# The state-space block's output projection merged with the norm, the turns and the routing logits that follow it

## The chip, the cores and the metric

The kernel runs on one core of one Trainium2 chip. The metric is the device time of one execution in microseconds (us). Five engines run their own instruction streams and meet at semaphores: PE (matmuls; PEld is its weight load, which overlaps it), DVE (vector), ACT (scalar), POOL (GpSimd) and SP (here it only issues DMAs).

## The reference, cut to what matters

Two layers act on x of 4 x 1024 tokens by 128 features. The second layer's first half is a state-space block, and its second half is a mixture of experts with 8 experts, of which each token takes 2. Around the change it computes:

```python
y = y * silu(z)                               # 256 inner features a token
out = y @ out_proj_w.T                        # 256 -> 128
out = out @ fc2_w.T + fc2_b                   # 128 -> 128
x = x + out
xn = layernorm(x)                             # over the 128 features, eps 1e-5
logits = xn @ gate_w.T + lb_bias              # 128 -> 8, then sigmoid, top 2
x = x + experts(xn, logits) + shared(xn)
```

## The kernel before, in words

All 4096 tokens stay in SBUF. `X` holds them with 128 tokens on the partitions, as 32 tiles of 128 features. `xnT` holds the normalized tokens turned, with the features on the partitions. The work goes by chunks of 512 tokens (4 tiles, one PSUM bank): `NCH` = 8 chunks, `CPB` = 2 chunks to a sequence of 1024 tokens, `TPC` = 4 tiles to a chunk, `TB` = 8 tiles to a sequence.

The program is a row of blocks. Each block gives every engine its list of instructions, and a block begins only when all engines have ended the one before. The last blocks are:

1. `mamba_scan` ends with two gates on DVE (L1907), which multiply the scan's sums by silu(z) into `m.u`.
2. `mamba_out`. PE multiplies the two output weights into one (L1960, `out_proj` by `fc2`), ACT copies the product to SBUF (L1974), and then PE makes each chunk's projection (L1967): 4 tiles x 2 halves of the inner features. In f32 each of these matmuls takes two passes, so a chunk has 16 of the trace's PE instructions. DVE adds a chunk to `X` (L1981) and takes its statistics, one `bn_stats` for each tile (L85). Two PSUM banks are used in turn. DVE runs in a loop over pairs of chunks.
3. `norm_transpose` of visit 2. SP issues the loads of the routing weights (L124, three tensors) and of the expert weights (three more). DVE turns the statistics of all 32 tiles into mean and variance + eps in seven small steps (L149 to L155). POOL raises the variance to the power -0.5 in eight pieces of 4 tiles (L134). DVE normalizes a chunk with four `tensor_scalar` (L164) into one of two halves of `xn`, PE turns it with four transposes (L177), and ACT copies the turned chunk to `xnT` (L209). One chunk behind, PE makes the routing logits of 8 columns (L183): 4 matmuls, 8 instructions in the trace.
4. `route_second` takes sigmoid and top 2 of the logits. Its first DVE instruction needs all of them, and stands in the next block.
5. `second_ffn` runs the experts, and ends the kernel.

In this part there is no planner: the order on each engine is the order in which the code above lists it. PE's and DVE's lists are worked in order, so that an instruction that waits holds up all that stand behind it.

In an earlier part of the kernel, between attention and the first layer's experts, the class `Front` already does a sum, statistics, moments, root and norm by sequence in straight code: L994 is its add, L85 its statistics, L1012 to L1022 its moments over 8 tiles, L984 the root of 8 tiles on POOL, L1030 the norm.

Of the kernel before, what the change touches and what calls it, by code (L numbers as in the profile page):

```python
# [11 lines left out]
ALU = mybir.AluOpType  # L12
# [76 lines left out]
LOGITS = 7  # L89


def norm_transpose(nc, g, visit, loads=(), load_x=False, route=None):

    with ExitStack() as ctx:
# [9 lines left out]
        steps_before = visit * STAT_STEPS  # L106
        if load_x:
            half_set, stats_ready = sem("half_set"), sem("stats_ready")
        if route is not None:
            logits_done = sem("logits_done")  # L110
        x_loaded = g.second_ring_in
        block = ctx.enter_context(nc.Block())

# [54 lines left out]
        @block.tensor  # L168
        def _(pe):
            pe.sem_inc(stored, TURNS)  # L170
            pe.wait_ge(g.consts_loaded, 32)

            def turn(c, k):
                pe.wait_ge(normed, chunks_before + c + 1)
                pe.wait_ge(stored, credits_before + c + 1)
                for j in range(TPC):
                    last = pe.transpose(PS[:, k, j * P:(j + 1) * P], xn[:, k, j, :], ident[:, :])  # L177
                last.then_inc(transposed, 1)

            def logits(c):  # L180
                pe.wait_ge(stored, credits_before + TURNS + c + 1)
                for n in range(c * TPC, (c + 1) * TPC):
                    last = pe.matmul(PS[:, LOGITS, n * n_experts:(n + 1) * n_experts], xnT[:, n * P:(n + 1) * P], route.gate_w[:, :],  # L183
                                     start=True, stop=True)
                last.then_inc(logits_done, 1)

            if route is None:
                with pe.Fori(0, NCH // TURNS) as i:
                    for k in range(TURNS):
                        turn(TURNS * i + k, k)  # L190
            else:

                n_experts = route.gate_w.shape[1]
                pe.wait_ge(route.loaded, route.all)
                for c in range(NCH):
                    turn(c, c % TURNS)
                    if c > 0:
                        logits(c - 1)
                logits(NCH - 1)
                pe.wait_ge(logits_done, NCH)  # L200

        @block.scalar
        def _(act):
# [701 lines left out]
class Front:  # L905
# [180 lines left out]
    def mix(self, pe, b, k):  # L1086
        c = CPB * b + k
        if c == 0:
            pe.wait_ge(self.wo_in, 16)
        if b == 2 and k == 0:  # L1090
            pe.wait_ge(self.route_steps, self.SCORES)
        if b >= 2 and k == 1:
            pe.wait_ge(self.added, c)
        if b == 3 and k == 0:
            pe.wait_ge(self.x_stored, c)
        pe.wait_ge(self.divided, c + 1)
        for j in range(TPC):
# [381 lines left out]
LOW_AT = (4 * NS, 6 * NS)  # L1479


def mamba_loads(nc, ctx, early, g):

    sb = lambda name, shape, dt=F32: ctx.enter_context(nc.sbuf_tensor(f"m_{name}", shape, dt))
    m = Loads(nc, ctx, "m_w")
    m.d = m.tensor("d", [P, DI], g.w["d"])
    m.last = Loads(nc, ctx, "mo_w")
    m.out_proj, m.fc2 = m.last.tensor("out_proj", [P, DI, P], g.w["out_proj"]), m.last.tensor("fc2", [P, E], g.w["fc2"])
    m.u, m.sz, m.dt = sb("u", [P, DI, N]), sb("sz", [P, DI, N]), sb("dt", [P, DI, N])
    m.dtu_turns = sb("dtu_turns", [P, NT, DI, P])  # L1490
# [12 lines left out]
    m.a_log = m.tensor("a_log", [P, DI, NS], g.w["a_log"])
    m.fc2_b = m.tensor("fc2_b", [P, E], g.w["fc2_b"].to_broadcast([P, E]))
    return m
# [435 lines left out]
                    pool.tensor_tensor(ch[:, half, :], decay_then_h(s, half), c_rows[:, s % C_RING, :], ALU.mult).then_inc(ch_ready, 1)  # L1941


def mamba_out(nc, g, m):

    with ExitStack() as ctx:
        sb = lambda name, shape, dt=F32: ctx.enter_context(nc.sbuf_tensor(f"mo_{name}", shape, dt))
        sem = lambda name: ctx.enter_context(nc.semaphore(f"mo_{name}"))
        X, PS = g.X, g.PS
        out_proj, fc2 = m.out_proj, m.fc2  # L1950
        w = sb("w", [P, DI, E])
        fused, w_ready, mixed, added, stats_ready = map(sem, ("fused", "w_ready", "mixed", "added", "stats_ready"))
        block = ctx.enter_context(nc.Block())

        @block.tensor
        def _(pe):
            pe.sem_inc(added, 2)
            pe.wait_ge(m.last.loaded, m.last.all)
            for half in range(DI):
                last = pe.matmul(PS[:, 2, half * E:(half + 1) * E], out_proj[:, half, :], fc2[:, :], start=True, stop=True)  # L1960
            last.then_inc(fused, 1)
            pe.wait_ge(w_ready, 1)
            for c in range(NCH):
                pe.wait_ge(added, c + 1)
                for j in range(TPC):
                    for half in range(DI):
                        last = pe.matmul(PS[:, c % 2, j * E:(j + 1) * E], m.u[:, half, c * CH + j * P:c * CH + (j + 1) * P], w[:, half, :],  # L1967
                                         start=half == 0, stop=half == DI - 1)
                last.then_inc(mixed, 1)

        @block.scalar
        def _(act):
            act.wait_ge(fused, 1)
            act.activation(w[:, :, :].rearrange("p a b -> p (a b)"), PS[:, 2, 0:DI * E], ACT.Copy).then_inc(w_ready, 1)  # L1974

        @block.vector
        def _(dve):
            def add(c, k):
                dve.wait_ge(mixed, c + 1)
                x = X[:, bass.ds(c * TPC, TPC), :]  # L1980
                dve.tensor_tensor(x, x, PS[:, k, :].rearrange("p (j e) -> p j e", e=E), ALU.add).then_inc(added, 1)  # L1981

            def stats(c):
                dve.wait_ge(added, 2 + c + 1)
                for j in range(TPC):
                    last = tile_stats(dve, g, c * TPC + j)
                last.then_inc(stats_ready, 1)

            with dve.Fori(0, NCH // 2) as i:
                for k in range(2):  # L1990
                    add(2 * i + k, k)
                    stats(2 * i + k)
            dve.wait_ge(stats_ready, NCH)

I2 = 64
PAIRS = NE // 2
# [267 lines left out]
def program(nc, w, out):  # L2264

    with ExitStack() as ctx:
        g = make_globals(nc, ctx, w, out)
        with ExitStack() as scope:
            first = first_loads(nc, scope, g)
            f = Front(nc, scope, g, first)  # L2270
            with ExitStack() as inner:
                weights = qkv_loads(nc, inner, g)
                norm_transpose(nc, g, 0, [weights], load_x=True)
                attention(nc, g, weights, f)
            first_ffn(nc, g, first, f)
        with ExitStack() as scope:
            with ExitStack() as early:
                m = mamba_loads(nc, scope, early, g)
                norm_transpose(nc, g, 1, [m, m.last])
                mamba_in(nc, g, m)  # L2280
            mamba_scan(nc, g, m)
            mamba_out(nc, g, m)
        with ExitStack() as scope:
            weights = second_loads(nc, scope, g)
            norm_transpose(nc, g, 2, [weights.route, weights], route=weights.route)
            route_second(nc, g, weights)
            second_ffn(nc, g, weights)

# [15 lines left out]
```

## Time and profile before

| | |
|---|---|
| median of 3 runs | 1384.82 us (1381.36 to 1385.63) |
| the profiled execution | 1387.3 us; span from first to last instruction 1385.5 us |
| mean granted TensorE clock | 0.933 |
| busy in the span | PE 1233.7, DVE 1089.5, ACT 851.2, POOL 575.9 us |
| last gate of the scan ends | 1215.02 us |
| last routing logits end | 1259.35 us |

Times are counted from the span's first instruction. "Idle before" in a timeline row, in square brackets, is how long the engine had stood idle before the row, and what ended that. "x16" is how many instructions the row merges. PEclk is the granted clock of TensorE: 1.00 is 2.4 GHz, 0.50 is 1.2 GHz. The first and third numbers of a windows row are the stretch and PE's busy time in it.

### The profile page before, as it was taken

The numbers are of one execution on the slowest core, as the hardware profiler recorded it, in microseconds if no ns is written. First come the engines' busy times: TensorE is split into PE (matmuls) and PEld (weight loads), VectorE is DVE, ScalarE is ACT, GpSimd is POOL, SyncE is SP. The second block draws the span as 40 slices with busy tenths as digits, with TensorE's granted clock in tenths as the row PEclk, the third lists the DMA queues.
The fourth block names the chain that finished last, engine by engine and source line by source line (L and its number), as shares of the span: only waits on it lengthen the run. The fifth ranks groups of instructions, "written<-read, shape, count | busy, mean of one in ns | idle before, by whom it ended". The sixth has DMA issues, their size and how long they took to land. (4 is left out here: it accounts for less than half of the span.)

```text
span 1385.5 us, 23363 instructions
## 1 busy us (share of the span) xinstructions
PE 1233.7 (89%) x8438; PEld 647.1 (47%) x8438; DVE 1089.5 (79%) x1318; ACT 851.2 (61%) x1506; POOL 575.9 (42%) x428
## 2 busy tenths in 40 slices
PE   4948999999899979899996966999999999976998
PEld 2412343333334435344443334655655556564665
DVE  4778999999799546856554867999999999864554
ACT  2524999999798633232222778989999899612221
POOL 2330000100111147666575024988888888820000
PEclk9966999999999889999996986999999999985999
DMA  4331112311211154332450001322222222110221
GB/s 112 103 126 43 55 51 66 104 57 52 79 43 43 42 125 139 97 103 94 117 103 22 0 6 48 106 92 92 100 99 92 92 99 100 61 29 22 63 62 38
DMA packets 70525, 103.16 MB, mean 74 GB/s; under 512 B 12598, under 2 KB 42246, under 8 KB 70422
## 3 DMA queue, kind: packets, MB, share of 16 engines
q1 hardware_dynamic: 69126, 100.47, 24.2%
q10 hardware_dynamic: 1296, 1.33, 0.3%
q8 instruction: 64, 1.05, 0.3%
q14 instruction: 39, 0.32, 0.1%
HBM read 88.00 MB, written 13.37 MB: 73 GB/s over the span
## 5 line engine op out<-in xcount | busy, mean ns | idle before, releaser
L646 DVE TENSOR_REDUCE att_found<-PS 128x2 f32<-128x1024 f32 (+2 forms) x288 | 333.0, 1219 | 15.1 <-PE PS L755 13.5
L722 ACT ACTIVATE att_prob<-PS 128x512 f32<-128x512 f32 x576 | 313.5, 596 | 44.5 <-PE PS L777 32.7
L1941 POOL TENSOR_TENSOR ms_ch<-xnT,ms_c_rows 128x1024 f32<-128x1024 f32 x103 | 243.9, 2369 | 45.1 <-PE PS L1851 33.1
L1851 PE MATMUL PS<-ms_ch,ident_sb 128*128 128x512 f32 x512 | 241.2, 593 | 0.9 <-POOL ms_ch L1941 0.9
L1902 DVE TENSOR_TENSOR_SCAN xnT<-xnT,PS 128x1024 f32<-128x1024 f32 x103 | 231.1, 2268 | 7.4 <-PE PS L1842 7.1
L1880 ACT ACTIVATE ms_scaled<-m_dtu_turns,m_bt 128x256 f32<-128x256 f32 x448 | 191.5, 495 | 29.3 <-PE PS L1842 29.3
L796 PE MATMUL PS<-att_prob,att_v 128*32 128x256 f32 (+1 forms) x2560 | 185.3, 376 | 2.8 <-ACT fr_out L711 2.6
L1842 PEld LDWEIGHTS PS<-ident_sb,ms_scaled 128*128 128x128 f32 x1024 | 120.5, 143 | 80.2 <-DVE xnT L1902 37.4
L1842 PE MATMUL PS<-ident_sb,ms_scaled 128*128 128x128 f32 x1024 | 136.8, 278 | 9.7 <-ACT ms_scaled L1880 4.6
L755 PE MATMUL PS<-kr,qr 55*128 55x128 bf16 (+4 forms) x1152 | 121.2, 291 | 25.2 <-DVE att_found L646 13.4
L1270 ACT ACTIVATE f_h<-PS,e_w_b 128x512 f32<-128x512 f32 x64 | 44.0, 687 | 140.7 <-PE PS L1421 137.4
L777 PE MATMUL PS<-qr,kr 55*128 55x128 bf16 (+4 forms) x1152 | 116.0, 279 | 10.3 <-ACT att_prob L722 7.4
L1851 PEld LDWEIGHTS PS<-ms_ch,ident_sb 128*128 128x128 f32 x512 | 87.3, 190 | 64.6 <-issue 61.2
L1887 ACT ACTIVATE xnT<-m_dt,m_a 128x1024 f32<-128x1024 f32 x103 | 116.8, 1135 | 0.0
L1251 POOL TENSOR_TENSOR f_yT<-f_yT,f_prod 128x512 f32<-128x512 f32 x56 | 71.1, 1269 | 75.2 <-DVE f_prod L1363 73.8
L755 PEld LDWEIGHTS PS<-kr,qr 48*128 48x128 bf16 (+1 forms) x1152 | 39.3, 96 | 133.6 <-issue 94.0
L1353 DVE SCALAR_TENSOR_TENSOR f_x3s<-PS,e_w_b,f_mask_row 128x512 f32<-128x512 f32 x64 | 48.0, 750 | 62.7 <-PE PS L1425 62.0
L1239 POOL TENSOR_TENSOR f_xm<-xnT,f_gate_row 128x512 f32<-128x512 f32 x64 | 81.2, 1271 | 11.4 <-DMA f_gate_row<-gate_rows_dram 7.5
L796 PEld LDWEIGHTS PS<-att_prob,att_v 128*32 128x32 f32 x2560 | 55.2, 109 | 64.1 <-issue 54.1
L1430 PE MATMUL PS<-f_h,e_w_w 128*128 128x512 f32 x128 | 66.3, 600 | 8.5 <-DVE f_prod L1363 8.4
L1421 PE MATMUL PS<-f_xm,e_w_w 128*128 128x512 f32 x128 | 67.6, 611 | 5.8 <-POOL f_xm L1239 5.8
L605 POOL TENSOR_TENSOR att_neg<-att_zero,att_row_max 128x32 f32<-128x32 f32 x16 | 4.1, 254 | 164.7 <-DVE att_row_max L659 164.7
(225 smaller groups left out, 1749.6 us busy)
## 6 DMA issues: line engine op xcount, KB each, us to landing
ms_c_rows<-bc_rows_dram SPq DMA_DIRECT2D x64, 512.0 KB, 3.6
f_gate_row<-gate_rows_dram SPq DMA_DIRECT2D x64, 256.0 KB, 3.4
f_mask_row<-mask_rows_dram SPq DMA_DIRECT2D x64, 128.0 KB, 3.1
qk_parts_dram<-parts SPq DMA_DIRECT2D x48, 128.0 KB, 1.9
heads_dram<-fr_out SPq DMA_DIRECT2D x16, 256.0 KB, 2.7
f_mask_row<-mask_rows_dram SPq DMA_DIRECT2D x64, 64.0 KB, 3.3
qr<-qk_parts_dram SPq DMA_DIRECT2D x32, 96.0 KB
qr<-qk_parts_dram SPq DMA_DIRECT2D x96, 32.0 KB
```

The costliest lines, as they stand in the source:

```text
L646: dve.tensor_reduce(found[:, :, pair, first:first + (n - 1) * step + 1:step], PS[:, bank:bank + 2, :].rearrange("p r (w n) -> p r w n", w= ...
L722: act.activation(prob[:, step % PROB_RING * GH + h, :], PS[:, SCORE_BANK + unit % SCORE_RING, :], ACT.Exp, scale=float(D) ** -0.5).then_in ...
L755: last = pe.matmul(PS[:, MAX_BANK + 2 * (m % 2) + r, at:at + n], rows(qr, count, i, pair, r, q_block * P, P), rows(kr, count, i, pair, r, ...
L777: last[r] = pe.matmul(PS[:, SCORE_BANK + (unit + r) % SCORE_RING, col:col + w], rows(kr, count, i, pair, r, j * P, P), rows(qr, count, i, ...
L796: last = pe.matmul(PS[VW * h:VW * (h + 1), VALUE_BANK, q - half * CH:q - half * CH + w], v1[:, i % 2, half, h, j, :], prob[:, step % PROB_ ...
L1239: pool.tensor_tensor(xm[:, e % XM_RING, :], xnT[:, c * CH:(c + 1) * CH], gate_row[:, e % ROW_RING, :], ALU.mult).then_inc(xm_ready, 1)
L1842: last = pe.transpose(PS[:, X_BANK + 2 * half + k // TPC, k % TPC * P:(k % TPC + 1) * P], scaled[:, s % 2, k, half, :], g.ident[:, :])
L1851: last = pe.matmul(PS[:, Y_BANK + 2 * half + q, :], g.ident[:, :], ch[:, half, q * CH:(q + 1) * CH], start=n == 0, stop=n == NS - 1)
L1880: last = act.activation(scaled[:, s % 2, i, :, :], m.dtu_turns[:, TB * b + i, :, :], ACT.Identity, scale=m.bt[:, at:at + 1])
L1887: act.activation(decay_then_h(s, half), m.dt[:, half, sequence(b)], ACT.Exp, scale=m.a[:, half, n:n + 1]).then_inc(decay_ready, 1)
L1902: dve.tensor_tensor_scan(decay_then_h(s, half), decay_then_h(s, half), inputs(half), 0.0, ALU.mult, ALU.add).then_inc(scanned, 1)
L1941: pool.tensor_tensor(ch[:, half, :], decay_then_h(s, half), c_rows[:, s % C_RING, :], ALU.mult).then_inc(ch_ready, 1)
```

## The change

`mamba_out` and `norm_transpose` of visit 2 become one block. The old visit-2 norm and its logits are no longer called, and `norm_transpose` loses its logits branch.

- **PE** runs, by steps 0 to 7, the projections of `BACK_MIXES` (chunks 0, 1, 2, 3 in step 0, then 4, 5, 6, 7 in steps 1 to 4), then the step's turn, then the logits of the chunk before. A projection of chunk c waits until chunk c-2 has been added to `X`.
- **DVE** runs in straight code: add and statistics of chunk c; after each second chunk the seven moment steps of that sequence (8 tiles, three of them without a wait behind them); then the norm of `BACK_NORMS`, which stands two chunks behind. After step 7 the norms of chunks 6 and 7 follow.
- **POOL** takes the root of one sequence's 8 tiles at a time: four instructions in place of eight.
- **ACT** copies each turned chunk to `xnT`, without the table load that the old norm began with.
- **SP** issues the six weight loads at the start of the merged block.
- The scan's tensors `sz`, `dt`, `dtu_turns`, `a` and `bt` are released before the merged block, so that the second layer's expert weights find room there.

```diff
+BACK_MIXES = [(0, 1, 2, 3), (4,), (5,), (6,), (7,), (), (), ()]
+BACK_NORMS = [(), (), (0,), (1,), (2,), (3,), (4,), (5,)]
...
+            def mix(c):
+                pe.wait_ge(w_ready, 1)
+                if c >= 2:
+                    pe.wait_ge(added, c - 1)
+                for j in range(TPC):
+                    for half in range(DI):
+                        last = pe.matmul(PS[:, c % 2, j * E:(j + 1) * E], m.u[:, half, c * CH + j * P:c * CH + (j + 1) * P], fused_w[:, half, :],
+                                         start=half == 0, stop=half == DI - 1)
+                last.then_inc(mixed, 1)
+
+            def turn(c):
+                pe.wait_ge(g.normed, norms_before + c + 1)
+                if c >= 2:
+                    pe.wait_ge(g.stored, turns_before + c - 1)
+                for j in range(TPC):
+                    last = pe.transpose(PS[:, TURN_BANK + c % 2, j * P:(j + 1) * P], xn[:, c % 2, j, :], g.ident[:, :])
+                last.then_inc(g.transposed, 1)
...
             for c in range(NCH):
-                pe.wait_ge(added, c + 1)
...
+                for ahead in BACK_MIXES[c]:
+                    mix(ahead)
+                if c == 1:
+                    pe.wait_ge(route.loaded, route.all)
+                turn(c)
+                if c >= 1:
+                    logits(c - 1)
+            logits(NCH - 1)
+            pe.wait_ge(logits_done, NCH)
...
+        @block.gpsimd
+        def _(pool):
+            for b in range(B):
+                pool.wait_ge(g.stat_steps, steps_before + STAT_STEPS * (b + 1))
+                pool.tensor_tensor(rstd[:, b % 2, :], tmp[:, 3, :], g.half[:, 0:TB], ALU.pow).then_inc(g.rstd_ready, 1)
...
+            for c in range(NCH):
+                add(c)
+                if c % CPB == CPB - 1:
+                    moments(c // CPB)
+                for ready in BACK_NORMS[c]:
+                    normalize(ready)
+            for c in (6, 7):
+                normalize(c)
...
-            mamba_scan(nc, g, m)
-            mamba_out(nc, g, m)
-        with ExitStack() as scope:
+                mamba_scan(nc, g, m)
             weights = second_loads(nc, scope, g)
-            norm_transpose(nc, g, 2, [weights.route, weights], route=weights.route)
+            mamba_out(nc, g, m, weights)
             route_second(nc, g, weights)
```

## Rows read from the trace of the kernel before

**Rows 1.** The page: its span, and the head of the chain that ended last.

```profile
span 1385.5 us, 23363 instructions
...
PE 8%; issue 0%; DVE 0%; PEldq 0%; DVEq 0%
```

**Rows 2.** Timeline of 1213 to 1260 us: start, length, engine, line, work, idle before.

```profile
1213.80 1.22 DVE L1907 TENSOR_TENSOR m_u<-PS,m_sz 128x1024 f32<-128x1024 f32 x1 [1.08 <-PE PS L1851]
...
1216.87 14.56 PE L1967 MATMUL PS<-mo_w,m_u 128*128 128x128 f32 x128 [0.47 <-ACT mo_w L1974]
1219.09 0.69 DVE L1981 TENSOR_TENSOR X<-X,PS 128x512 f32 x1 [4.07 <-PE PS L1967]
...
1234.61 0.33 SPq L124 DMA_DIRECT2D r_w_gate_w<-gate  x1
...
1234.76 0.21 DVE L149 TENSOR_TENSOR norm_tmp<-stats 128x32 f32<-128x32 f32 x1 [0.61 <-PEq L1946]
...
1236.43 8.09 POOL L134 TENSOR_TENSOR norm_rstd<-norm_tmp,half 128x4 f32<-128x4 f32 x8 [24.70 <-DVE norm_tmp L155]
...
1237.81 2.28 DVE L164 TENSOR_SCALAR norm_xn<-X,norm_mean,norm_rstd 128x128 f32 x8 [1.47 <-POOL norm_rstd L134]
...
1239.18 2.08 PE L177 MATMUL PS<-ident_sb,norm_xn 128*128 128x128 f32 x8 [7.76 <-DVE norm_xn L164]
...
1252.38 0.90 PEld L177 LDWEIGHTS PS<-ident_sb,norm_xn 128*128 128x128 f32 x4
...
1254.83 0.90 PEld L177 LDWEIGHTS PS<-ident_sb,norm_xn 128*128 128x128 f32 x4
...
1255.93 3.42 PE L183 MATMUL PS<-r_w_gate_w,xnT 128*128 128x8 f32 x16
```

**Rows 3.** Timeline of 447 to 457 us, DVE and then POOL: the like in the front.

```profile
447.77 0.69 DVE L994 TENSOR_TENSOR X<-X,PS 128x512 f32<-128x512 f32 x1 [1.81 <-PE PS L1098]
...
449.28 0.67 DVE L994 TENSOR_TENSOR X<-X,PS 128x512 f32<-128x512 f32 x1
...
450.89 0.17 DVE L1012 TENSOR_TENSOR fr_moments_tmp<-stats 128x8 f32<-128x8 f32 x1
...
454.19 2.14 DVE L1030 TENSOR_SCALAR fr_xn<-X,fr_mean,fr_rstd 128x128 f32<-128x128 f32 x8 [1.90 <-POOL fr_rstd L984]
...
452.43 1.65 POOL L984 TENSOR_TENSOR fr_rstd<-fr_moments_tmp,half 128x8 f32<-128x8 f32 x1 [5.69 <-DVE fr_moments_tmp L1022]
```

**Rows 4.** Windows: stretch, busy time of PE, PEld, DVE, ACT, POOL, PEclk, DMA, GB/s.

```profile
1216.00:1231.00 15.00, 14.53 (x130) 14.34 (x129) 10.32 (x31) 0.39 (x1) 0.00 (x0) 1.00 0.00 1
1236.00:1237.00 1.00, 0.00 (x0) 0.00 (x0) 0.31 (x2) 0.00 (x0) 0.57 (x1) 0.52 0.19 9
1240.00:1259.00 19.00, 19.00 (x94) 18.66 (x92) 6.78 (x25) 4.78 (x8) 4.52 (x5) 0.50 0.04 16
```

**Rows 5.** Timeline of PE at 585, 590, 788 and 861 us: bursts after a pause.

```profile
585.75 1.10 PE L1430 MATMUL PS<-f_h,e_w_w 128*128 128x512 f32 x2 [2.21 <-DVE f_prod L1363]
...
590.04 1.18 PE L1430 MATMUL PS<-f_h,e_w_w 128*128 128x512 f32 x2 [1.89 <-DVE f_prod L1363]
...
788.01 2.93 PE L1731 MATMUL PS<-xnT,mi_w_in_x 128*128 x4 [2.03 <-ACT mi_xc L1597]
...
861.48 2.87 PE L1842 MATMUL PS<-ident_sb,ms_scaled 128*128 128x128 f32 x12 [0.20 <-ACT ms_scaled L1880]
```

**Rows 6.** Windows beside rows 5: granted clock (PEclk) in the stretches there.

```profile
586.00:589.00 3.00, 2.15 (x8) 0.79 (x7) 3.00 (x4) 0.60 (x1) 2.24 (x2) 1.00 0.40 129
591.00:594.00 3.00, 3.00 (x5) 1.35 (x4) 1.44 (x2) 0.00 (x0) 3.00 (x4) 0.50 0.32 108
789.00:792.00 3.00, 3.00 (x5) 1.35 (x4) 3.00 (x7) 2.24 (x5) 0.00 (x0) 0.50 0.00 0
793.00:796.00 3.00, 3.00 (x8) 1.32 (x7) 3.00 (x7) 1.93 (x5) 0.00 (x0) 1.00 0.00 0
864.00:865.00 1.00, 1.00 (x5) 0.57 (x4) 1.00 (x2) 1.00 (x2) 1.00 (x1) 1.00 0.00 0
```

More of the change, by code:

```diff
@@ L89, with norm_transpose @@
 LOGITS = 7
-def norm_transpose(nc, g, visit, loads=(), load_x=False, route=None):
+def norm_transpose(nc, g, visit, loads=(), load_x=False):
     with ExitStack() as ctx:
@@ L108, in norm_transpose @@
             half_set, stats_ready = sem("half_set"), sem("stats_ready")
-        if route is not None:
-            logits_done = sem("logits_done")
         x_loaded = g.second_ring_in
@@ L178, in turn @@
                 last.then_inc(transposed, 1)
[L180 to L200, printed above, removed]
+            with pe.Fori(0, NCH // TURNS) as i:
+                for k in range(TURNS):
+                    turn(TURNS * i + k, k)
         @block.scalar
@@ L1479, with mamba_loads @@
 LOW_AT = (4 * NS, 6 * NS)
-def mamba_loads(nc, ctx, early, g):
+def mamba_loads(nc, ctx, scan, early, g):
     sb = lambda name, shape, dt=F32: ctx.enter_context(nc.sbuf_tensor(f"m_{name}", shape, dt))
@@ L1488, in mamba_loads @@
     m.out_proj, m.fc2 = m.last.tensor("out_proj", [P, DI, P], g.w["out_proj"]), m.last.tensor("fc2", [P, E], g.w["fc2"])
-    m.u, m.sz, m.dt = sb("u", [P, DI, N]), sb("sz", [P, DI, N]), sb("dt", [P, DI, N])
+    m.u = sb("u", [P, DI, N])
+    sb = lambda name, shape, dt=F32: scan.enter_context(nc.sbuf_tensor(f"m_{name}", shape, dt))
+    m.sz, m.dt = sb("sz", [P, DI, N]), sb("dt", [P, DI, N])
     m.dtu_turns = sb("dtu_turns", [P, NT, DI, P])
@@ L1941, in _, with mamba_out @@
                     pool.tensor_tensor(ch[:, half, :], decay_then_h(s, half), c_rows[:, s % C_RING, :], ALU.mult).then_inc(ch_ready, 1)
-def mamba_out(nc, g, m):
+BACK_MIXES = [(0, 1, 2, 3), (4,), (5,), (6,), (7,), (), (), ()]
+BACK_NORMS = [(), (), (0,), (1,), (2,), (3,), (4,), (5,)]
+def mamba_out(nc, g, m, w):
     with ExitStack() as ctx:
@@ L1948, in mamba_out @@
         sem = lambda name: ctx.enter_context(nc.semaphore(f"mo_{name}"))
-        X, PS = g.X, g.PS
+        X, PS, xnT, stats, route = g.X, g.PS, g.xnT, g.stats, w.route
         out_proj, fc2 = m.out_proj, m.fc2
-        w = sb("w", [P, DI, E])
-        fused, w_ready, mixed, added, stats_ready = map(sem, ("fused", "w_ready", "mixed", "added", "stats_ready"))
-        block = ctx.enter_context(nc.Block())
+        fused_w = sb("w", [P, DI, E])
+        tmp = sb("tmp", [P, 4, TB])
+        mean, rstd = sb("mean", [P, 2, TB]), sb("rstd", [P, 2, TB])
@@ new lines, in mamba_out, with _ @@
+        xn = sb("xn", [P, 2, TPC, E])
+        fused, w_ready, mixed, added, stats_ready, logits_done = map(sem, ("fused", "w_ready", "mixed", "added", "stats_ready", "logits_done"))
+        visit = 2
+        steps_before, roots_before, norms_before = visit * STAT_STEPS, visit * NCH, visit * NCH
+        turns_before = visit * (NCH + TURNS)
+        FUSED_BANK, TURN_BANK = 2, 3
+        block = ctx.enter_context(nc.Block())
+        @block.sync
+        def _(sp):
+            for group in (w.route, w):
+                for dst, src in group.pairs:
+                    sp.dma_start(dst, src).then_inc(group.loaded, 16)
@@ L1955, in _ @@
         @block.tensor
         def _(pe):
-            pe.sem_inc(added, 2)
+            def mix(c):
[7 more added lines that the diff above has]
+                last.then_inc(mixed, 1)
@@ new lines, in turn, with logits @@
+            def turn(c):
[5 more added lines that the diff above has]
+                last.then_inc(g.transposed, 1)
+            def logits(c):
+                pe.wait_ge(g.stored, turns_before + c + 1)
+                n_experts = route.gate_w.shape[1]
+                for n in range(c * TPC, (c + 1) * TPC):
+                    last = pe.matmul(PS[:, LOGITS, n * n_experts:(n + 1) * n_experts], xnT[:, n * P:(n + 1) * P], route.gate_w[:, :], start=True, stop=True)
+                last.then_inc(logits_done, 1)
@@ L1958, in _ @@
             pe.wait_ge(m.last.loaded, m.last.all)
             for half in range(DI):
-                last = pe.matmul(PS[:, 2, half * E:(half + 1) * E], out_proj[:, half, :], fc2[:, :], start=True, stop=True)
+                last = pe.matmul(PS[:, FUSED_BANK, half * E:(half + 1) * E], out_proj[:, half, :], fc2[:, :], start=True, stop=True)
             last.then_inc(fused, 1)
-            pe.wait_ge(w_ready, 1)
             for c in range(NCH):
-                pe.wait_ge(added, c + 1)
[L1965 to L1969, printed above, removed]
+                for ahead in BACK_MIXES[c]:
+                    mix(ahead)
@@ L1973, in _, with add @@
             act.wait_ge(fused, 1)
-            act.activation(w[:, :, :].rearrange("p a b -> p (a b)"), PS[:, 2, 0:DI * E], ACT.Copy).then_inc(w_ready, 1)
+            act.activation(fused_w[:, :, :].rearrange("p a b -> p (a b)"), PS[:, FUSED_BANK, 0:DI * E], ACT.Copy).then_inc(w_ready, 1)
+            for c in range(NCH):
+                act.wait_ge(g.transposed, turns_before + c + 1)
+                act.activation(xnT[:, c * CH:(c + 1) * CH], PS[:, TURN_BANK + c % 2, :], ACT.Copy).then_inc(g.stored, 1)
+            act.wait_ge(g.stored, turns_before + NCH)
+        @block.gpsimd
[3 more added lines that the diff above has]
+                pool.tensor_tensor(rstd[:, b % 2, :], tmp[:, 3, :], g.half[:, 0:TB], ALU.pow).then_inc(g.rstd_ready, 1)
         @block.vector
         def _(dve):
-            def add(c, k):
+            def add(c):
                 dve.wait_ge(mixed, c + 1)
[L1980 to L1984, printed above, removed]
+                x = X[:, c * TPC:(c + 1) * TPC, :]
+                dve.tensor_tensor(x, x, PS[:, c % 2, :].rearrange("p (j e) -> p j e", e=E), ALU.add).then_inc(added, 1)
+                dve.wait_ge(added, c + 1)
                 for j in range(TPC):
@@ L1987, in stats, with moments, normalize @@
                 last.then_inc(stats_ready, 1)
[L1989 to L1993, printed above, removed]
+            def moments(b):
+                steps = Steps(dve, g.stat_steps, steps_before + STAT_STEPS * b)
+                me, qe, mo, qo = (stats[:, TB * b:TB * (b + 1), k] for k in (1, 2, 4, 5))
+                dve.wait_ge(stats_ready, CPB * (b + 1))
+                if b > 0:
+                    dve.wait_ge(g.rstd_ready, roots_before + b)
+                steps.mark(dve.tensor_tensor(tmp[:, 0, :], me, mo, ALU.add))
+                steps.mark(dve.tensor_tensor(tmp[:, 1, :], me, mo, ALU.subtract))
+                steps.done(dve.tensor_tensor(tmp[:, 2, :], qe, qo, ALU.add))
+                steps.done(dve.scalar_tensor_tensor(tmp[:, 1, :], tmp[:, 1, :], 0.25, tmp[:, 1, :], ALU.mult, ALU.mult))
+                steps.mark(dve.scalar_tensor_tensor(tmp[:, 2, :], tmp[:, 2, :], 1.0 / E, tmp[:, 1, :], ALU.mult, ALU.add))
+                steps.done(dve.tensor_scalar(mean[:, b % 2, :], tmp[:, 0, :], 0.5, None, ALU.mult))
+                steps.done(dve.tensor_scalar(tmp[:, 3, :], tmp[:, 2, :], EPS, None, ALU.add))
+            def normalize(c):
+                b = c // CPB
+                dve.wait_ge(g.rstd_ready, roots_before + b + 1)
+                if c >= 2:
+                    dve.wait_ge(g.transposed, turns_before + c - 1)
+                for j in range(TPC):
+                    n = c % CPB * TPC + j
+                    last = dve.tensor_scalar(xn[:, c % 2, j, :], X[:, c * TPC + j, :], mean[:, b % 2, n:n + 1], rstd[:, b % 2, n:n + 1],
+                                             ALU.subtract, ALU.mult)
+                last.then_inc(g.normed, 1)
+            for c in range(NCH):
+                add(c)
[5 more added lines that the diff above has]
+                normalize(c)
+            dve.wait_ge(g.normed, norms_before + NCH)
 I2 = 64
@@ L2276, in program @@
         with ExitStack() as scope:
[L2277 to L2280, printed above, removed]
-            mamba_scan(nc, g, m)
-            mamba_out(nc, g, m)
-        with ExitStack() as scope:
+            with ExitStack() as scan:
+                with ExitStack() as early:
+                    m = mamba_loads(nc, scope, scan, early, g)
+                    norm_transpose(nc, g, 1, [m, m.last])
+                    mamba_in(nc, g, m)
+                mamba_scan(nc, g, m)
             weights = second_loads(nc, scope, g)
-            norm_transpose(nc, g, 2, [weights.route, weights], route=weights.route)
+            mamba_out(nc, g, m, weights)
             route_second(nc, g, weights)
```

## The prediction

> **What bounds the kernel now.** I read the page first. The span is 1385.5 us, and the chain that ended last lies wholly in the last block: its steps are PE's, 8% of the span [rows 1]. The blocks before it are joined by barriers, so the chain cannot be followed back through them. But for the same reason each block's length counts in full. So the second view is the timeline from the scan's last gate to the last routing logits, which are the two ends between which the change works. The gate ends at 1213.80 + 1.22 = 1215.02, the logits at 1255.93 + 3.42 = 1259.35 [rows 2]. The stage takes 44.3 us, 3.2% of the span, and nothing outside it is touched.
>
> The reader should see three parts in it. First the projections: PE's 128 passes in 14.56 us, 0.114 us each and 1.82 us a chunk, with DVE's add starting 2.22 us after its chunk [rows 2]. PE is through at 1231.4. Then a stretch in which PE has nothing: 7.76 us, in which the last statistics, the barrier, the moments, the first root and the first norm follow one another [rows 2]. Then turns and logits, PE busy for 19.00 of 19 us. The third view, windows, tells why this part is long: the granted clock was 1.00 during the projections, fell to 0.52 in the microsecond from 1236, in the pause, and stood at 0.50 from 1240 to 1259 [rows 4]. So 19 us of such work at 1.2 GHz did not bring 2.4 GHz back. A chunk of turn and logits takes 1254.83 - 1252.38 = 2.45 us [rows 2], where 12 passes at the full clock's 0.114 would take 1.37.
>
> **The change part by part.** I count from the gate's end, t = 0. What is removed: one barrier (0.61 us of idle before L149), the pause of PE, and seven moment steps on 32 columns. What is added: moments four times on 8 columns, and roots of 8 tiles. Their prices come from the front's rows, the same work in straight code [rows 3]. Add and statistics of a chunk: 449.28 - 447.77 = 1.51 us, 1.61 ahead of moments; I take 1.6. Moments: 1.54 from the first step to the root, of which 0.1 is the hand-over; three waits fewer leave 1.3 (bounds 1.2, which is seven times 0.17, and 1.45). Root of 8 tiles: 1.65, and the norm starts 0.11 behind it. Norm of a chunk: 2.14 / 2 = 1.07.
>
> DVE's whole list is then 8 x 1.6 + 4 x 1.3 + 8 x 1.07 = 26.6 us, PE's at the full clock 8 x (1.82 + 1.37) = 25.5. Neither is far from the other, so the waits decide. In order of the lists, with 0.2 from a norm to its turn and 0.4 from a projection's last pass to its add (2.22 - 1.82):
>
> PE projects chunks 0 to 3 from 1.85 to 9.1. DVE: adds at 4.1 and 5.9, moments 7.5 to 8.8, add 2, root in POOL 8.9 to 10.5, norm 0 from 10.7 to 11.8. PE, which is in order, has turn 0 ahead of projection 4: it stands from 9.1 to 12.0, and projects chunk 4 from 12.4 to 14.2. DVE: add 3, moments, norm 1 until 15.7. PE: turn 1 at 15.9, logits 0, projection 5 until 19.1. DVE is free at 18.4 and waits for it until 19.5: a new wait of 1.1, caused by norm 1 -> turn 1 -> projection 5 -> add 5, and queued behind that add are moments 2 and norm 3. Add 5, moments 2 and norm 3 end at 23.5. PE stood from 22.3 to 23.7; turn 3, logits 2, projection 7 until 26.8. DVE waits again, from 26.1 to 27.2. Add 7, moments 3 and norm 5 end at 31.2. PE stands from 28.2, turns chunk 5 at 31.4. At the full clock norms 6 and 7 end at 33.1 and 34.2, and turns and logits at 37.1. This bound gives 44.3 - 37.1 = 7.2 us of gain.
>
> Moved at no cost: the six loads. They are issued at t = 0.6 and the logits' wait is reached at 14.2; before, they were issued from 1234.61 on and the same wait was passed by the turns at 1239.18 [rows 2], so 4.6 us are enough; without that cover it would be up to 4.6. No queue on SP stands behind them in this block. The table load of ACT goes; it lay beside the moments.
>
> **The clock decides what is kept.** The new tail, from 28.2 on, is a pause of 3.2 us and then turns and logits alone, the work at which the clock stood at 0.50 for 19 us [rows 4]. I take it at half: turn 5 at 31.4, two more chunks at 2.45, then from a last turn to the end 1259.35 - 1254.83 = 4.5 [rows 2]: 40.8. The gain is 3.5.
>
> In the middle the pauses are 2.9, 1.7 and 1.4 us with the logits' small columns beside them. At other places a burst after a pause of 2.03 us (788.01) and one of 1.89 (590.04) was followed by the clock at 0.50 for the next microseconds, and after a pause of 2.21 (585.75) it stayed at 1.00 [rows 5, 6]. So a pause of 2.9 us will most likely cost the clock, those of 1.7 and 1.4 may. It then took 3 to 4 us of full work at half speed until it was back (789 to 792 at 0.50, 793 to 796 at 1.00) [rows 6], about one projection of 3.64. A projection at half is 1.82 longer. For chunks 5 and 7 all of it is added, since DVE waits for them; for 4 and 6, where DVE comes 1.1 and 0.8 later than the result, 0.7 and 1.0 of it. I take one projection's 1.82 in all (bounds nothing and two, 3.6). Sum: -3.5 + 1.8 = -1.7, with own range -3.5 to +0.1.
>
> The Trainium skill, "TensorE: Matmul & The Clock Gate", Part 4, says that transposes do not bring the full clock about, since they don't count as busy in the same way. The trace differs: from 861.48 PE had only transposes, 2.87 us of them, and the clock was 1.00 from 864 on [rows 5, 6]. By the page's rule the four turns would never help the clock between projections, and two projections rather than one would go at half: +0.1 in place of -1.7. That lies within the own range above, so it is no rival of its own.
>
> **The rivals.** Kept clock: if the pauses in the middle and at the end do not cost it, the stage ends at 37.1, a change of -7.2, or -5 with half a tail. For it speaks that 2.21 us did not; against it that 3.2 us at the end are more than any pause here that left the clock alone.
>
> Lost clock, the other side: it falls at the pause before turn 0 and does not return, because pauses and 8-column work stand between the projections, as from 1240 to 1259. Turn 0 ends at 12.7, projection 4 at 16.3, and each further chunk takes 3.64 + 2.45 = 6.1: projection 7 ends at 34.6. Add, moments and norm 5 lead to 39.1, the tail of 4.9 + 4.5 to 48.5: +4.2 us. It decides from the third late projection on: two times 1.8 use up the 3.5. Against it: between 12.0 and 16.3 PE would be full without a pause, and full work brought the clock back by 793 and by 864 [rows 6].
>
> No effect of the merging: DVE's straight code costs as much as the loops did (1.9 a chunk instead of 1.6, which was paced by PE there). Then 5 further adds of 0.3 are on the path, 1.5 us, and the sum is -0.2: the own range again.
>
> **How the numbers follow.** The profiled execution took 1387.3 us, 2.5 above the median of 1384.8. Its sum with the change is 1385.6, and by the median 1384.8 - 1.7 = 1383.1. Chances: forecast with its own range 0.67, kept clock 0.15, lost clock 0.10, and 0.08 for what none of these names, in either direction. 0.3% is 4.2 us, about what a measurement of this kernel can tell from no change. Faster by more: kept clock, most of it, and a tail of the forecast: 0.18. Slower by more: half of lost clock and some of the unnamed: 0.08. Within: 0.74. The range leaves out half of the kept clock and most of the lost one: 1378.5 to 1388.
>
> **What would show it.** Right: PE's pause before turn 0 near 3 us; DVE's waits for L1967's successor at chunks 5 and 7; four roots of 1.65; last logits 41 to 44 us after the gate; PEclk at 0.5 in the last ten microseconds of them, and at 0.5 for 3 to 4 us once in the middle. Wrong: a last logits below 39 us (the clock was kept, or comes back in the tail), or above 47 with PEclk at 0.5 through projections 4 to 7; or a DVE chunk of add and statistics at 1.9 in straight code.

## The result, and the profile after

The changed kernel took 1378.42 us, median of 10 runs (1376.26 to 1383.94), against 1385.34 for 10 runs of the kernel before (1381.36 to 1389.27). The ratio is 0.9958 with a 95% interval of 0.9944 to 0.9973, which is 5.8 us less (3.7 to 7.8). The forecast was 1383.1, 1.7 less than the 1384.8 that it started from, with a range of 1378.5 to 1388. As ratios these are 0.9988 and 0.9954 to 1.0023, so the result is inside, at the low end. The chance given to faster by over 0.3% was 0.18. Ratios, here and below, leave out three executions that took 1.5 to 4.8 times as long: two of the twelve of e1, and one of the 23 of the kernel before that ran beside e1 to e4.

In the profiled executions the span fell by 10.3 us, from 1385.5 to 1375.2. That has to be split before it is read. The last gate ends at 1207.85 + 1.22 = 1209.07, 5.95 earlier, in blocks that the change leaves alone; in the profiles of the experiments below, whose earlier blocks are the same too, it ended anywhere from 1208.15 to 1215.04. From gate to last logits, the stage, it is 38.66 us against 44.33: 5.67 less. Behind the logits it is 127.47 against 126.15. Most of that 1.3 us is the clock at the start of the expert block: it came back to 1.00 about 3 us behind that block's first expert matmul before (1274.05, at 1.00 from 1277 on), and about 5.5 us behind it after (1262.45, at 1.00 from 1268 on). In the experiments below this part took 126.34 to 127.66. So the stage's 5.67 is as much as the 5.8 us that the runs show, and I compare the stage from here on.

The timeline of the stage after. L1962 is the projection, L1971 the turn, L1978 the logits; L2016 the add, L2028 to L2034 the moments, L2043 the norm, L2009 the root:

```profile
1207.85 1.22 DVE L1889 TENSOR_TENSOR m_u<-PS,m_sz 128x1024 f32<-128x1024 f32 x1 [1.08 <-PE PS L1833]
...
1210.78 7.41 PE L1962 MATMUL PS<-mo_w,m_u 128*128 128x128 f32 x64 [0.47 <-ACT mo_w L1999]
...
1212.87 0.69 DVE L2016 TENSOR_TENSOR X<-X,PS 128x512 f32<-128x512 f32 x1 [3.79 <-PE PS L1962]
...
1216.28 0.17 DVE L2028 TENSOR_TENSOR mo_tmp<-stats 128x8 f32<-128x8 f32 x1
1216.37 0.17 DVE L2029 TENSOR_TENSOR mo_tmp<-stats 128x8 f32<-128x8 f32 x1
...
1217.35 0.69 DVE L2016 TENSOR_TENSOR X<-X,PS 128x512 f32<-128x512 f32 x1
1217.39 1.65 POOL L2009 TENSOR_TENSOR mo_rstd<-mo_tmp,half 128x8 f32<-128x8 f32 x1 [11.61 <-DVE mo_tmp L2034]
...
1219.07 1.11 DVE L2043 TENSOR_SCALAR mo_xn<-X,mo_mean,mo_rstd 128x128 f32<-128x128 f32 x4
...
1220.24 0.66 PE L1971 MATMUL PS<-ident_sb,mo_xn 128*128 128x128 f32 x4 [2.05 <-DVE mo_xn L2043]
...
1224.06 0.63 PE L1971 MATMUL PS<-ident_sb,mo_xn 128*128 128x128 f32 x4 [1.37 <-DVE mo_xn L2043]
...
1227.40 0.69 DVE L2016 TENSOR_TENSOR X<-X,PS 128x512 f32<-128x512 f32 x1 [0.98 <-PE PS L1962]
...
1231.26 0.66 PE L1971 MATMUL PS<-ident_sb,mo_xn 128*128 128x128 f32 x4 [0.78 <-DVE mo_xn L2043]
...
1234.64 0.69 DVE L2016 TENSOR_TENSOR X<-X,PS 128x512 f32<-128x512 f32 x1 [0.91 <-PE PS L1962]
...
1237.37 1.64 POOL L2009 TENSOR_TENSOR mo_rstd<-mo_tmp,half 128x8 f32<-128x8 f32 x1 [5.60 <-DVE mo_tmp L2034]
...
1238.50 1.12 PE L1971 MATMUL PS<-ident_sb,mo_xn 128*128 128x128 f32 x4 [2.67 <-DVE mo_xn L2043]
1239.04 2.14 DVE L2043 TENSOR_SCALAR mo_xn<-X,mo_mean,mo_rstd 128x128 f32<-128x128 f32 x8 [0.60 <-POOL mo_rstd L2009]
...
1243.22 0.90 PEld L1971 LDWEIGHTS PS<-ident_sb,mo_xn 128*128 128x128 f32 x4
...
1244.31 3.42 PE L1978 MATMUL PS<-r_w_gate_w,xnT 128*128 128x8 f32 x16
```

They answer to [rows 2]. The 7.76 us pause of PE is gone; in its place there are pauses of 2.05 before turn 0 (1220.24), 1.37 and 0.78 before turns 1 (1224.06) and 3 (1231.26), and 2.67 before turn 5 (1238.50). DVE waits for projections 5 and 7, 0.98 (1227.40) and 0.91 us (1234.64), and for the last root 0.60 (1239.04). From turn 5 to the end it is 9.23 us: two chunks in 4.93, and 4.30 from the last turn (1243.43) to the end. The windows say at which clock:

```profile
1210.00:1236.00 26.00, 21.15 (x183) 20.33 (x182) 20.13 (x81) 3.37 (x6) 4.92 (x3) 1.00 0.14 39
1237.00:1238.00 1.00, 0.00 (x0) 0.00 (x0) 0.93 (x6) 0.00 (x0) 0.63 (x1) 0.60 0.00 0
1238.00:1247.70 9.70, 9.20 (x44) 9.14 (x44) 2.58 (x10) 1.79 (x3) 1.01 (x1) 0.50 0.01 3
```

The clock stayed at 1.00 through all eight projections, with their pauses, and fell in the pause before turn 5. The tail went at 0.50, as [rows 4] did over all eight chunks.

### The profile page after: what moved, and what is told of

The parts are those of the page before. It is cut to its first block and busy times, and to the rows that moved or that the text cites. A ratio compares the mean times of both kernels' runs of the same rounds, so it can differ in the third digit from the quotient of the medians.

```text
span 1375.2 us, 23176 instructions
## 1 busy us (share of the span) xinstructions
PE 1223.8 (89%) x8438; PEld 641.1 (47%) x8438; DVE 1090.1 (79%) x1339; ACT 849.8 (62%) x1505; POOL 573.9 (42%) x424
## 5 line engine op out<-in xcount | busy, mean ns | idle before, releaser
L2239 ACT ACTIVATE f_sg<-PS 128x512 f32<-128x512 f32 x40 | 23.9, 597 | 78.5 <-PE PS L2222 78.5
```

## The experiments

Two theories at first. A: the gain is the filled pause; five of eight chunks are turned while the clock is up, and DVE's list and the waits on PE's order set where the tail starts. B: the gain is the merging, that is the barrier, the loops and the small roots. The stage times, with what was expected, come from one profile each; the ratio is to the kernel before, with its 95% interval:

| kernel | stage us | expected | ratio of the whole |
|---|---|---|---|
| before | 44.33 | | 1 |
| changed | 38.66 | 42.6 | 0.9958 (0.9944 to 0.9973) |
| e1 no stagger | 42.14 | 42.5 | 0.9981 (0.9965 to 0.9997) |
| e2 warm tail | 36.71 | 35.3 to 36 | 0.9939 (0.9918 to 0.9960) |
| e3 no lag | 42.03 | 42.3 | 0.9987 (0.9972 to 1.0002) |
| e4 short tail | 36.60 | 36.8 | 0.9943 (0.9924 to 0.9963) |
| e5 three ahead | 65.64 | 50 to 67 | one run, 1407.16 us |
| e6 five ahead | 36.42 | 36.8 | 0.9950 (0.9933 to 0.9966) |
| e7 five and short | 34.70 | 34.7 to 35.1 | 0.9948 (0.9932 to 0.9965) |
| e8 the same, warm | 33.36 | 33.3 | 0.9924 (0.9908 to 0.9940) |

A ratio's interval is some 2 us to either side. It tells e8 from the changed kernel, e1 and e3 nearly, and e2, e4, e6 and e7 not. For e3 it does not exclude the time of the kernel before. For all these the verdict rests on the stage, in one profile.

**e1: merged, but not staggered.**

```diff
-BACK_MIXES = [(0, 1, 2, 3), (4,), (5,), (6,), (7,), (), (), ()]
-BACK_NORMS = [(), (), (0,), (1,), (2,), (3,), (4,), (5,)]
+BACK_MIXES = [(0, 1, 2, 3, 4, 5, 6, 7), (), (), (), (), (), (), ()]
+BACK_NORMS = [(), (), (), (), (), (), (), ()]
...
-            for c in (6, 7):
+            for c in range(NCH):
                 normalize(c)
```

(`mean` and `rstd` are then held for all four sequences.)

> The merged block as changed (one block, straight code on DVE, moments and roots by sequence), but all eight projections, adds and statistics come first and all eight norms, turns and logits after them. Theory A (the gain is that PE's pause is filled, so that five of the eight chunks are turned at 2.4 GHz between projections): the stage from the last gate to the last logits ends at about 42.5 us, since PE pauses from 16.5 to 20.8, the clock falls, and the eight chunks go at 2.45 us each; that is 1.8 us less than before (44.33) and 3.8 more than the changed kernel (38.66). Theory B (the gain is the merging itself: a barrier, loops and the eight small roots gone): it ends near 39, within 0.5 us of the changed kernel.

PE's timeline:

```profile
1223.30 3.81 PE L1962 MATMUL PS<-mo_w,m_u 128*128 128x128 f32 x32 [0.37 <-DVE X L2016]
1232.02 2.21 PE L1971 MATMUL PS<-ident_sb,mo_xn 128*128 128x128 f32 x8 [4.91 <-DVE mo_xn L2043]
1234.02 1.71 PE L1978 MATMUL PS<-r_w_gate_w,xnT 128*128 128x8 f32 x8
...
1248.74 3.42 PE L1978 MATMUL PS<-r_w_gate_w,xnT 128*128 128x8 f32 x16
```

PE stood for 4.91 us, and all turns and logits behind went at half speed: 2.45 us a chunk again. The gate was at 1210.02, the end 42.14 behind it. So the merging alone is worth 2.2 of the 5.67 us, and the staggering the other 3.5. Theory B alone is out: it wanted 39.

**e2: the tail kept warm.**

```diff
+WARM = [0, 0, 0, 0, 6, 2, 1, 0]
...
+            def warm(n):
+                for _ in range(n):
+                    pe.matmul(PS[:, 5, 0:DI * E], g.ident[:, :], fused_w[:, :, :].rearrange("p a b -> p (a b)"), start=True, stop=True)
...
                 if c >= 1:
                     logits(c - 1)
+                warm(WARM[c])
```

> The changed kernel with PE kept busy in the tail: six, two and one idle matmuls (identity by the 256 columns of the fused weight, into an unused bank, 0.43 us each at 2.4 GHz) after the logits of chunks 3, 4 and 5. Nothing reads them. Theory A (the tail is long because the clock is at 0.50 in it): the granted clock stays at 1.00 to the last logits, and the stage ends at 35.3 to 36 us, about 3 less than the changed kernel's 38.66; the whole time falls by about 3 us or 0.2%. Rival (the tail is bound by the norms and by the latency of root, norm, turn and copy, not by PE's rate): the clock stays up but the end moves by less than 1 us, or later by the 0.4 to 0.8 us that the idle matmuls stand in front of turn 5.

Windows, PE's timeline and DVE's adds:

```profile
1216.00:1224.00 8.00, 4.58 (x41) 4.23 (x39) 7.52 (x31) 0.82 (x2) 3.28 (x2) 1.00 0.00 0
...
1225.00:1228.00 3.00, 3.00 (x17) 3.00 (x17) 1.09 (x3) 0.00 (x0) 0.00 (x0) 0.55 0.00 0
...
1235.00:1244.80 9.80, 9.80 (x71) 8.88 (x69) 5.38 (x24) 2.39 (x4) 1.64 (x1) 1.00 0.00 1
```

```profile
1219.31 0.66 PE L1972 MATMUL PS<-ident_sb,mo_xn 128*128 128x128 f32 x4 [2.05 <-DVE mo_xn L2049]
...
1223.12 0.63 PE L1972 MATMUL PS<-ident_sb,mo_xn 128*128 128x128 f32 x4 [1.37 <-DVE mo_xn L2049]
...
1224.39 2.97 PE L1963 MATMUL PS<-mo_w,m_u 128*128 128x128 f32 x16
...
1235.68 2.84 PE L1984 MATMUL PS<-mo_w,ident_sb 128*128 128x256 f32 x12
...
1242.95 1.91 PE L1979 MATMUL PS<-r_w_gate_w,xnT 128*128 128x8 f32 x16
```

```profile
1227.40 0.69 DVE L2022 TENSOR_TENSOR X<-X,PS 128x512 f32<-128x512 f32 x1 [1.91 <-PE PS L1963]
...
1234.63 0.69 DVE L2022 TENSOR_TENSOR X<-X,PS 128x512 f32<-128x512 f32 x1 [0.80 <-PE PS L1963]
```

The tail went at 1.00 (1235 to 1244.8) and took 6.36 us from turn 5 (1238.50) to the end instead of 9.23: 2.9 less, as expected. But the stage gained only 1.95, and the windows tell why. In this execution the clock fell in the middle, at about 1225.3, in projection 5, behind the pauses of 2.05 and 1.37 us before turns 0 and 1. The instructions up to there are those of the changed kernel, which had the same two pauses and kept its clock. Projection 5 took 2.97 us instead of 2.03, and add 5 waited 1.91 instead of 0.98: 0.93 us, the price of the lost clock that my sum had at 1.82. Without it the stage would be 35.8, an estimate from these rows, in the expected span.

**e3: norms right behind their moments.**

```diff
-BACK_NORMS = [(), (), (0,), (1,), (2,), (3,), (4,), (5,)]
+BACK_NORMS = [(), (0, 1), (), (2, 3), (), (4, 5), (), (6, 7)]
...
-            for c in (6, 7):
-                normalize(c)
```

> The changed kernel with the norms of a sequence's two chunks right behind its moments, instead of two chunks behind their projection. Theory A: DVE stands idle for each of four roots (1.65 + 0.1 us, of which the changed kernel shows only the last, 0.60), 4 x 1.75 = 7.0 us in all, of which 3.6 are added to the end, since the changed kernel's own waits of DVE for projections (0.98 and 0.91) and its last one go: stage 42.3 us, against 38.66. Theory B (the lag is not what matters): within 0.5 us of 38.66.

DVE's waits in the stage (total, times, longest), and a projection of PE:

```profile
DVE mo_xn L2043 <- POOL mo_rstd L2009: 7.3, 4, 1.8
```

```profile
1230.71 3.65 PE L1962 MATMUL PS<-mo_w,m_u 128*128 128x128 f32 x16 [0.27 <-DVE X L2016]
```

Four waits of 1.8 us for the root, 7.3 in all, and a stage 3.4 us longer than the changed kernel's. The lag of two chunks is there to hide POOL's 1.65 us root, and it is worth as much as the whole staggering. The clock fell in the middle here too: the projection at 1230.71 took 3.65 us, and the granted clock was 0.50 from 1231 to 1234. It cost nothing, since DVE waited for no projection behind the first two.

**e4: a shorter tail.**

```diff
-BACK_NORMS = [(), (), (0,), (1,), (2,), (3,), (4,), (5,)]
+BACK_NORMS = [(), (), (0,), (1,), (2,), (3,), (4, 5), ()]
+BACK_LOGITS = [(), (0,), (1,), (2,), (3,), (4, 5), (), (6, 7)]
...
-                if c >= 1:
-                    logits(c - 1)
-            logits(NCH - 1)
+                for back in BACK_LOGITS[c]:
+                    logits(back)
```

> The changed kernel with norm 5 moved ahead of add 7 (where DVE stood for 0.91 us) and the logits of chunk 5 ahead of turn 6, those of 6 behind turn 7. Theory A (from add 7 on, the end is set by statistics, moments, root, norm 6 and then PE's list at 1.2 GHz): turn 5, logits 4 and 5 go while PE would stand, and only turns 6 and 7 and logits 6 and 7 stay behind norm 6: about 5.3 us behind a norm 6 that ends 31.4 us after the gate, so the stage ends at 36.8, 1.9 less than 38.66. Rival (PE's total of half-speed work sets the end, and the clock falls earlier in the new order): not below 38.

PE's timeline of the end:

```profile
1238.65 0.64 PE L1972 MATMUL PS<-ident_sb,mo_xn 128*128 128x128 f32 x4
1239.12 1.91 PE L1979 MATMUL PS<-r_w_gate_w,xnT 128*128 128x8 f32 x16
1243.27 2.15 PE L1972 MATMUL PS<-ident_sb,mo_xn 128*128 128x128 f32 x8 [2.24 <-DVE mo_xn L2043]
1245.20 3.45 PE L1979 MATMUL PS<-r_w_gate_w,xnT 128*128 128x8 f32 x16
```

Turn 5 and the logits of chunks 4 and 5 (1238.65, 1239.12) went before the pause, at the full clock; behind norm 6 only two turns and two chunks of logits are left, 5.38 us. The stage lost 2.06.

**e5 and e6: three and five projections ahead instead of four.**

```diff
-BACK_MIXES = [(0, 1, 2, 3), (4,), (5,), (6,), (7,), (), (), ()]
+BACK_MIXES = [(0, 1, 2), (3,), (4,), (5,), (6,), (7,), (), ()]      # e5
+BACK_MIXES = [(0, 1, 2, 3, 4), (5,), (6,), (7,), (), (), (), ()]    # e6
```

> The changed kernel with one projection fewer ahead of turn 0: chunks 0, 1, 2 first, chunk c + 3 in step c. Theory A (a projection stands on PE behind the turn of an older chunk, which waits for that chunk's norm on DVE, so add c waits for norm c-3 and all that follows it): from chunk 3 on each add waits for 0.2 hand-over, turn 0.46, logits 0.91, projection 1.82 and 0.3 behind the norm just before it, so that a chunk takes about 3.7 + 1.5 + 1.05 = 6.3 us and one with moments 7.3. The stage ends near 50 us after the gate if the clock stays at 2.4 GHz and as late as 67 if it falls, against 38.66. Rival (the order of PE's list matters little, since DVE is the busier engine): below 41.

> The changed kernel with one projection more ahead of turn 0: chunks 0 to 4 first, chunk c + 4 in step c. Theory A: the pause of PE before turn 0 (2.05 us) is filled by projection 4 and the two waits of DVE for projections 5 and 7 (0.98 and 0.91) go, so that turn 5 starts 1.9 us earlier; the tail, still at 1.2 GHz, is as long as before: stage 36.8 us, 1.9 less than 38.66. Rival (the projections run out earlier, so the clock falls earlier and more turns go at half speed, which gives the gain back): 38.5 or more.

With three ahead, DVE's waits for projections (total, times, longest), some of its timeline, and PE's last logits:

```profile
DVE X L2016 <- PE PS L1962: 32.6, 7, 6.3
```

```profile
1230.02 1.12 DVE L2043 TENSOR_SCALAR mo_xn<-X,mo_mean,mo_rstd 128x128 f32<-128x128 f32 x4
1237.26 0.69 DVE L2016 TENSOR_TENSOR X<-X,PS 128x512 f32<-128x512 f32 x1 [6.12 <-PE PS L1962]
...
1238.77 1.10 DVE L2043 TENSOR_SCALAR mo_xn<-X,mo_mean,mo_rstd 128x128 f32<-128x128 f32 x4
1245.97 0.69 DVE L2016 TENSOR_TENSOR X<-X,PS 128x512 f32<-128x512 f32 x1 [6.10 <-PE PS L1962]
```

```profile
1274.36 3.42 PE L1978 MATMUL PS<-r_w_gate_w,xnT 128*128 128x8 f32 x16
```

Add 4 (1237.26) waits 6.12 us behind norm 1 (1230.02), and add 5 6.10 behind norm 2. From add 4 on the four waits are 5.96 to 6.33 us, longer than the 3.7 that was estimated for the full clock: the clock fell in PE's pauses, and the five late projections took 3.08 to 3.76 us instead of 2.03. The gate ended at 1212.14 and the last logits at 1277.78. So one projection too few in front of turn 0 costs 27.0 us in the stage, near the upper end of what was expected. The whole agrees within 2 us: this one run is 23.3 us above the median of the kernel before beside it (1383.89), and its stage 21.3 above. With five ahead, PE and one window:

```profile
1216.74 9.43 PE L1962 MATMUL PS<-mo_w,m_u 128*128 128x128 f32 x80 [0.47 <-ACT mo_w L1999]
1226.21 0.66 PE L1971 MATMUL PS<-ident_sb,mo_xn 128*128 128x128 f32 x4
...
1242.42 0.92 PE L1971 MATMUL PS<-ident_sb,mo_xn 128*128 128x128 f32 x4 [2.27 <-DVE mo_xn L2043]
...
1248.04 3.42 PE L1978 MATMUL PS<-r_w_gate_w,xnT 128*128 128x8 f32 x16
```

```profile
1242.04:1243.04 1.00, 0.62 (x4) 0.62 (x5) 0.40 (x3) 0.00 (x0) 0.89 (x1) 0.82 0.00 0
```

The five projections run through (80 passes), turn 0 follows at once, DVE has no wait for projections 5 and 7, and turn 5 comes at 1242.42 - 1215.04 = 27.4 behind the gate instead of 29.4. The stage lost 2.24. The rival, that the clock would fall earlier and take the gain back, did not come about: it fell just behind the start of turn 5, 27.6 us behind the gate, and in the changed kernel in the pause before turn 5, 28.1 behind the gate. In both the tail from turn 5 on went at 0.50, but for the first of it in e6.

**e7: both, and a root in two pieces.**

```diff
             for b in range(B):
                 pool.wait_ge(g.stat_steps, steps_before + STAT_STEPS * (b + 1))
-                pool.tensor_tensor(rstd[:, b % 2, :], tmp[:, 3, :], g.half[:, 0:TB], ALU.pow).then_inc(g.rstd_ready, 1)
+                for k in range(CPB):
+                    part = slice(k * TPC, (k + 1) * TPC)
+                    pool.tensor_tensor(rstd[:, b % 2, part], tmp[:, 3, part], g.half[:, part], ALU.pow).then_inc(g.rstd_ready, 1)
```

(With five ahead and the order of e4; DVE's waits count the pieces.)

> Five projections ahead, norm 5 ahead of add 7, logits 5 ahead of turn 6 and 6 behind turn 7, and POOL's root in two pieces of 4 tiles, so that norm 6 needs only the first (about 1.05 us where the whole took 1.65). Theory A: the short tail gave 2.06 of stage time, the fifth projection gives what its own run shows (about 1, since norm 5 in DVE's wait was part of the short tail's gain), the first root 0.6: stage 34.7 to 35.1 us where the clock is kept in the middle, up to 36.5 where it is not. Rival (the gains share one slack and do not add up): 36 or more in a run whose middle is at 1.00.

A window, and PE's end:

```profile
1235.54:1236.54 1.00, 1.00 (x10) 1.00 (x9) 0.99 (x3) 0.60 (x1) 0.00 (x0) 0.83 0.00 0
```

```profile
1240.85 2.14 PE L1972 MATMUL PS<-ident_sb,mo_xn 128*128 128x128 f32 x8 [0.21 <-DVE mo_xn L2045]
1242.79 3.45 PE L1979 MATMUL PS<-r_w_gate_w,xnT 128*128 128x8 f32 x16
```

The stage is 34.70, 1.9 below e4 and 1.7 below e6, as was expected. The gains share some slack all the same: e4's 2.06 and e6's 2.24 alone would make 4.3, the split root brings norm 6 another 0.6 (DVE waits 1.18 for it instead of 1.81), and together they gave 3.96. The clock fell earlier than in e6, at 1236.2, 24.7 us behind the gate and behind a pause of only 1.02 us; turn 5 and the logits of chunks 4 and 5 went at half speed. It cost nothing, since PE was through 0.21 us before turn 6 could start (1240.85). The whole time (0.9948) does not show it beside e4's 0.9943: the difference is less than either interval, and one profile does not tell in how many runs the clock fell early.

**e8: e7 with PE kept busy in its pauses.**

```diff
+WARM = [0, 0, 0, 2, 3, 4, 1, 0]
...
                 for back in BACK_LOGITS[c]:
                     logits(back)
+                warm(WARM[c])
```

> The kernel of the run before with two, three, four and one idle matmuls of 0.43 us behind the logits of steps 3, 4, 5 and 6, in PE's pauses. Nothing reads them. Theory A (turns 6 and 7 and logits 6 and 7 go at 1.2 GHz otherwise): the clock stays at 1.00 to the end and the stage ends at 33.3 us, 1.3 less than without them; the whole time is about 2 us under that of the warm tail alone. Rival (the idle matmuls delay the turns by as much as the clock gives): equal to the run without them, or later.

The whole stage in one window, and PE's end:

```profile
1210.00:1242.80 32.80, 31.10 (x248) 29.32 (x248) 24.20 (x100) 5.16 (x9) 8.05 (x8) 1.00 0.11 32
```

```profile
1237.82 1.97 PE L1985 MATMUL PS<-mo_w,ident_sb 128*128 128x256 f32 x8
1239.63 0.60 PE L1973 MATMUL PS<-ident_sb,mo_xn 128*128 128x128 f32 x4
...
1240.93 1.93 PE L1980 MATMUL PS<-r_w_gate_w,xnT 128*128 128x8 f32 x16
```

The clock was 1.00 from 1210 to the last logits at 1242.86. The stage took 33.36 us, 1.34 less than e7, where 1.3 was expected. This version takes 10.5 us less than the kernel before (8.3 to 12.7), and its interval lies wholly, if barely, below that of the changed kernel (0.9940 against 0.9944).

## Why the prediction was right in direction and too small in size

**What held.** The gain lies in the stage, and the tail goes at half speed: turn 5 to the end 9.4 expected, 9.23 measured. PE's pause before turn 0 was put at 2.9 and is 2.05; DVE's two new waits, at 1.1 each, are 0.98 and 0.91, and e5 and e6 show that they come by the chain norm, turn, projection, add. The loads cost nothing: turn 1, the first instruction behind PE's wait for them, was released by norm 1 (1224.06). The root was put at 1.65 and took 1.65. That the clock matters was right: e2 got 2.9 us for it at the tail.

The prediction's own signs say that it was off. Of its signs of being right, a last logits 41 to 44 us behind the gate and a clock at 0.5 once in the middle did not come; its first sign of being wrong, a last logits below 39 us, did, at 38.66. That the whole time is still in the range is partly luck: a gain of 5.8 us is outside the forecast's own -3.5 to +0.1, and the range reached that far only because it took in part of the kept clock rival.

**What failed.** Two terms of the sum were mis-sized, with nearly equal weight.

First, "I take one projection's 1.82 in all" for a clock lost in the middle. In the changed kernel's profile it was nothing, all projections at 1.00; where the same instructions lost it, in e2, it was 0.93: projection 5 was half done when the clock fell (0.94 us longer is 8 of its 16 passes at 0.114 more), and what came late behind it was taken up in PE's pause before turn 3. The bound of nothing stood in the text, and gave -3.5; I chose the middle between two ends that the rows did not tell apart.

Second, the start of the tail: "PE stands from 28.2, turns chunk 5 at 31.4"; measured 29.43. Most of it lies in the prices of DVE's steps. The moments took 1.07 us from first step to the next instruction (1216.28 to 1217.35), not 1.3: behind the three steps without a wait the next one starts 0.085 us later (1216.28, 1216.37), not 0.17 (I had taken away a wait but left the duration). Four times 0.23 is 0.9. Add 0 starts 3.80 behind the gate and not 4.1, 0.3. Norm 0 started 0.03 us behind its root (1217.39 + 1.65; 1219.07), where the sum had 0.2: another 0.2. From turns 1 and 3 to adds 5 and 7 it took 3.34 and 3.38 us (1224.06 to 1227.40, 1231.26 to 1234.64), where the sum had 3.6 and 3.5: 0.4. Together 1.8 of the 2.0; the rest is rounding in hand-overs. So the end without a lost clock was 40.8 in my sum and 38.66 on the chip.

The two add to 1.8 + 2.1 = 3.9, within rounding the distance from -1.7 to -5.67. "Kept clock" had named a gain of 5 "with half a tail" as a rival; what came is near it in number only: a kept clock in the middle and the whole tail at half, with DVE faster than priced.

The rule that transposes do not count for the clock (the Trainium skill, "TensorE: Matmul & The Clock Gate", Part 4) was not tested apart. The middle kept its clock with turns between the projections, and lost it once with the same turns.

**Open.** How often the middle loses its clock in the changed kernel. One profile in which it did (e2) and two in which it did not (the changed kernel, e4), with the same instructions up to that point, is all that these runs show. Two profiles of other orders, e3 and e7, lost it before the last turns as well. Each stage time is from one profile, so a stage time of e1 to e8 holds for the clock that this one execution had.

## What to carry to other kernels

When a stage is re-ordered, write down the waits from the lists before any gain: with PE in order, a projection behind a turn waits for that turn's norm, and one projection more or fewer ahead (e6, e5) moved the stage by -2.2 or +27.0 us. Price steps of one engine by their pitch where they do not wait on one another, not by their duration. And where PE is left with work of few columns behind a pause, fill the pause: ten idle matmuls of 0.43 us gave 1.3 us here (e8), and the clock was 2.4 GHz through the whole stage.

## What the runs showed of the hardware that was not expected

The same instructions with the same two pauses of PE (2.05 and 1.37 us) kept the clock at 1.00 in two executions (the changed kernel, e4) and were followed by 0.55 in a third (e2, 1225 to 1228). In e7 the clock fell behind a pause of 1.02 us, and in e6 it stayed up behind the same pause. So the rows support no more than a chance for the clock behind pauses of this length.

Small DVE operations on 128 x 8 last 0.17 us each, yet start 0.085 us apart when nothing is waited for (1216.28, 1216.37, 1216.45 in the changed kernel) and 0.20 us apart where each waits for the one before (450.89, 451.10, 451.30 in the front). A root of 128 x 4 takes 1.0 us on POOL (e7: two in 2.00) and one of 128 x 8 1.65, so that splitting it brings its first half 0.6 us earlier and takes 0.35 more in all.
